# One-hot dispatch tables in paired 16-bit columns, and a semaphore for the first block's rows

## The reference, cut to what matters

```python
for j in range(C):                     # layer 0: two rounds
    gate = (xf @ router_W[j] + router_b[j]) / TEMP
    _, ids = jax.lax.top_k(gate + gate_bias[j], TOPK)          # TOPK = 2
    sel = (ids[:, :, None] == jnp.arange(E)[None, None, :]).any(axis=1)
    weights = softmax(where(sel, gate, -inf))
    ...                                # experts, weighted sum, shared experts, rms norm
# layer 1
gate_scores, expert_idx = jax.lax.top_k(tokens @ gate_w.T, 2)
out = sum over experts of c[:, e] * (gelu(tokens @ W1[e].T + B1[e]) @ W2[e].T + B2[e])
```

## Time and profile before

| | us |
|---|---|
| median of 3 runs | 1989.68 (1987.65 to 1990.22) |
| profiled execution, its own time | 1987.42 |
| its span | 1985.6 |
| TensorE busy (matmul) | 1745.8, 88% |
| VectorE busy | 1407.0, 71% |
| ScalarE busy | 1031.1, 52% |
| GpSimd busy | 828.3, 42% |
| mean granted clock of TensorE | 0.944 |

### The profile page before, as it was taken

How to read it: one execution, slowest core, us unless ns; L and a number is a source line. 1 busy time by engine, 2 the same in 40 slices (tenths; PEclk the granted TensorE clock), 3 DMA queues, 4 the chain that set the end, 5 groups by cost and what they waited for, 6 DMA issues and landing times. The chain is left out here.

```text
span 1985.6 us, 31822 instructions
## 1 busy us (share of the span) xinstructions
PE 1745.8 (88%) x11154; PEld 1543.6 (78%) x11154; DVE 1407.0 (71%) x2519; ACT 1031.1 (52%) x2084; POOL 828.3 (42%) x868
## 2 busy tenths in 40 slices
PE   5899999999999989999959899998389793999990
PEld 4788888888888878888848788887267682999990
DVE  4665465456434988777757987776799787788876
ACT  4344334334323434655555355554587462888882
POOL 2132232232222114777721257776231141888840
PEclk9999999999998999999979999999699885999995
DMA  4100000000012331666653236664700023788858
GB/s 159 64 1 11 11 5 5 11 11 0 11 57 93 110 114 55 211 191 197 196 175 124 76 112 192 194 185 152 250 33 1 1 75 122 232 276 274 268 176 264
DMA packets 147065, 233.01 MB, mean 117 GB/s; under 512 B 28162, under 2 KB 103172, under 8 KB 141956
## 3 DMA queue, kind: packets, MB, share of 16 engines
q1 hardware_dynamic: 123332, 167.04, 25.7%
q0 software_dynamic: 23616, 64.52, 10.9%
HBM read 175.65 MB, written 55.33 MB: 116 GB/s over the span
## 5 line engine op out<-in xcount | busy, mean ns | idle before, releaser
L183 POOL TENSOR_TENSOR spare_g<-neg_half 128x1 f32<-128x1 f32 x80 | 22.9, 287 | 577.6 <-ACT a_sg L553 141.3
L172 PE MATMUL bank<-gT_hi,w_hi 128*128 128x512 f32 x592 | 244.5, 413 | 0.0
L172 PE MATMUL bank<-gT_hi,w_lo 128*128 128x512 f32 x592 | 235.9, 398 | 0.0
L172 PE MATMUL bank<-gT_lo,w_hi 128*128 128x512 f32 x592 | 234.9, 397 | 0.0
L1817 POOL DMA_INDIRECT got<-b_rows,b_gather_i x168 | 170.7, 1016 | 65.8 <-issue 50.6
L1607 DVE TENSOR_TENSOR gT_lo<-bank,gT_hi 128x512 fp32r<-128x512 f32 x148 | 97.0, 690 | 132.7 <-ACT gT_hi L1430 102.4
L1460 ACT ACTIVATE m_hi<-gs 128x512 fp32r<-128x512 f32 x116 | 73.0, 633 | 124.1 <-DVE gs L1614 67.6
L172 PE MATMUL bank<-w_hi,m_hi 128*128 128x256 f32 x464 | 131.2, 283 | 5.2 <-DVE sent L1636 5.2
L172 PEld LDWEIGHTS bank<-gT_hi,w_lo 128*128 128x128 f32 x592 | 112.4, 190 | 27.2
L172 PE MATMUL bank<-w_lo,m_hi 128*128 128x256 f32 x464 | 131.0, 282 | 0.0
L172 PE MATMUL bank<-w_hi,m_lo 128*128 128x256 f32 x464 | 130.7, 282 | 0.0
(11 more groups left out here) (455 smaller groups left out, 5721.4 us busy)
## 6 DMA issues: line engine op xcount, KB each, us to landing
v_raw<-in_units SPq DMA_DIRECT2D x39, 1024.0 KB, 5.3
w_raw<-in_units SPq DMA_DIRECT2D x56, 256.0 KB, 4.0
shared<-in_units SPq DMA_DIRECT2D x40, 256.0 KB, 3.4
b_rows<-x SPq DMA_DIRECT2D x16, 512.0 KB, 3.1
got<-b_rows SPq DMA_DIRECT2D x16, 512.0 KB, 4.4
close_back<-b_kept SPq DMA_DIRECT2D x16, 512.0 KB, 6.2
d_back<-d_kept SPq DMA_DIRECT2D x16, 512.0 KB, 8.7
w_raw<-b_folded SPq DMA_DIRECT2D x26, 256.0 KB, 4.3
```

The lines of the kernel that those rows point to most:

```text
L172: ins = pe.matmul(out, a, b, start=first and n == 0, stop=last and n == of - 1)
L183: eng.tensor_tensor(b.spare_g[:, i:i + 1], b.neg_half[:, 0:1], b.neg_half[:, 0:1], ALU.mult)
```

## The change

Numbers and tables of the dispatch get a new layout and a new type. The 16 columns of a quarter are 8 runs of 2 (HOT_RUNS, HOT_RUN), and each table is laid out [partition, run, number, 2], so that the same number of two neighbouring columns lies side by side. The column numbers 0 to 127 and 0 to 83 are kept as bf16 and doubled (`iota_h`, `iotaq_h`), the turn numbers as bf16 (`turn_h`), and `in_h`, `at_h` are bf16. All three products of a quarter are made by VectorE: hot_at, hot_in, and the whole turn half of hot_id. GpSimd's hot is gone in layer 0, and so are ScalarE's single-column activations in layer 1. TensorE reads the tables with a step of two elements. Three conversions are added to `tables_vector`. In layer 1 the first two gathers, block 0's rows, signal `first_rows`, for which turn(0) waits.

```diff
-TURN_COLS = 8
+HOT_RUN, HOT_RUNS = 2, PICKS * N // P // 8
+def hot_numbers(table):
+    return table.unsqueeze(1).broadcast_to([P, HOT_RUNS, table.shape[1], HOT_RUN])
+def hot_cols(values, n):
+    return values.rearrange("p (a b) -> p a b", b=HOT_RUN).unsqueeze(2).broadcast_to([P, HOT_RUNS, n, HOT_RUN])
...
@@ b_tensor, inverse @@
-            ins = pe.matmul(B[6][:, 0:2 * NQB], b.hot_in[:, col, :], b.hot_id[:, col, :, :].rearrange("p a q -> p (a q)"), start=col == 0, stop=col == COLS // 4 - 1)
+            run, at = col // HOT_RUN, col % HOT_RUN
+            ins = pe.matmul(B[6][:, 0:2 * NQB], b.hot_in[:, run, :, at], b.hot_id[:, run, :, :, at].rearrange("p a q -> p (a q)"), start=col == 0, stop=col == COLS // 4 - 1)
...
@@ tables_vector @@
+    v.tensor_copy(b.iota_h, spread(b.disp[:, DISP["iota"]], HOT_RUN)).then_inc(link.sem, 1)
+    v.wait_ge(link.sem, link.next())
+    v.tensor_copy(b.iotaq_h, spread(b.disp[:, DISP["iotaq"]], HOT_RUN)).then_inc(link.sem, 1)
+    v.wait_ge(link.sem, link.next())
+    v.tensor_copy(b.turn_h, b.disp[:, DISP["turn"]]).then_inc(link.sem, 1)
+    v.wait_ge(link.sem, link.next())
...
@@ hot_vector @@
-    v.tensor_tensor(b.hot_at[:, :, :], mid(b.disp[:, DISP["iotaq"]][:, 0:NQB], COLS // 4), spread(b.at_f[:, cs], NQB), ALU.is_equal).then_inc(r.hot_at.sem, 1)
-    v.tensor_tensor(b.hot_in[:, :, :], mid(b.disp[:, DISP["iota"]], COLS // 4), spread(b.in_f[:, cs], P), ALU.is_equal).then_inc(r.hot_in.sem, 1)
+    v.tensor_tensor(b.hot_at, hot_numbers(b.iotaq_h[:, 0:NQB, :]), hot_cols(b.at_h[:, cs], NQB), ALU.is_equal).then_inc(r.hot_at.sem, 1)
+    v.tensor_tensor(b.hot_in, hot_numbers(b.iota_h), hot_cols(b.in_h[:, cs], P), ALU.is_equal).then_inc(r.hot_in.sem, 1)
+    v.wait_ge(r.hot_at.sem, r.hot_at.at(4 * rnd + j))
+    v.tensor_tensor(b.hot_id[:, :, 0], b.hot_at, hot_cols(b.turn_h[:, cs], NQB), ALU.mult).then_inc(r.hot_turn.sem, 1)
...
@@ b_gpsimd @@
-        g.tensor_tensor(b.hot_id[:, :, 0, :], b.hot_at[:, :, :], spread(b.disp[:, DISP["turn"]][:, cs], NQB), ALU.mult).then_inc(r.hot_turn.sem, 1)
-    for j in range(4):
-        hot(j)
...
@@ dispatch_vector: the same three operations, for all 16 columns of a quarter @@
-        v.tensor_tensor(b.hot_id[:, mine, 0, :], b.hot_at[:, mine, :], spread(table("turn")[:, mine], nq), ALU.mult).then_inc(r.hot_turn.sem, 1)
+        v.tensor_tensor(b.hot_id[:, runs, 0], b.hot_at[:, runs], hot_cols(b.turn_h[:, cs], nq), ALU.mult).then_inc(r.hot_turn.sem, 1)
...
@@ dispatch_scalar @@
-        for col in range(cs.start + TURN_COLS, cs.stop):
-            act.activation(b.hot_id[:, col, 0, :], b.hot_at[:, col, :], ACT.Copy, scale=float(col))
...
@@ d_gpsimd, gathers @@
-            g.indirect_dma_start(b.got[n % 6][:, c, :], None, rows, bass.IndirectOffsetOnAxis(b.gather_i[:, q:q + 1], 0)).then_inc(r.gathered[n % 6].sem, 16)
+            landed = r.first_rows if q < QBD else r.gathered[n % 6]
+            g.indirect_dma_start(b.got[n % 6][:, c, :], None, rows, bass.IndirectOffsetOnAxis(b.gather_i[:, q:q + 1], 0)).then_inc(landed.sem, 16)
...
@@ d_tensor, turn @@
-        pe.wait_ge(r.gathered[n % 6].sem, r.gathered[n % 6].at(n // 6, 16 * gathers_of(n)))
+        if k == 0:
+            pe.wait_ge(r.first_rows.sem, r.first_rows.at(0))
+        else:
+            pe.wait_ge(r.gathered[n % 6].sem, r.gathered[n % 6].at(n // 6, 16 * gathers_of(n)))
```

More of the change, by code:

```diff
@@ L1463, in hot_part @@
         act.wait_ge(r.hot_at.sem, r.hot_at.at(4 * rnd + j))
-        act.activation(b.hot_id[:, :, 1, :], b.hot_at[:, :, :], ACT.Copy, scale=b.disp[:, DISP["p1"]]).then_inc(r.hot_part.sem, 1)
+        act.activation(b.hot_id[:, :, 1], b.hot_at, ACT.Copy, scale=b.disp[:, DISP["p1"]]).then_inc(r.hot_part.sem, 1)
     for j, now, after, third in turn_steps(rnd):
@@ L1803, in b_gpsimd @@
 def b_gpsimd(g, b, s, r, dram, rnd):
-    def hot(j):
-        cs = slice(j * COLS // 4, (j + 1) * COLS // 4)
-        g.wait_ge(r.hot_at.sem, r.hot_at.at(4 * rnd + j))
-        g.tensor_tensor(b.hot_id[:, :, 0, :], b.hot_at[:, :, :], spread(b.disp[:, DISP["turn"]][:, cs], NQB), ALU.mult).then_inc(r.hot_turn.sem, 1)
     def gathers(k):
@@ L2460, in dispatch_tensor @@
         for col in range(j * COLS // 4, (j + 1) * COLS // 4):
-            ins = pe.matmul(b.bank[2][:, 0:2 * nq], b.hot_in[:, col, :], b.hot_id[:, col, :, :].rearrange("p a q -> p (a q)"), start=col == 0, stop=col == COLS - 1)
+            run, at = col // HOT_RUN, col % HOT_RUN
+            ins = pe.matmul(b.bank[2][:, 0:2 * nq], b.hot_in[:, run, :, at], b.hot_id[:, run, :, :, at].rearrange("p a q -> p (a q)"), start=col == 0, stop=col == COLS - 1)
     ins.then_inc(r.inverse.sem, 1)
@@ L2466, in dispatch_scalar @@
     for j in range(4):
-        cs = slice(j * COLS // 4, (j + 1) * COLS // 4)
+        runs = slice(j * HOT_RUNS, (j + 1) * HOT_RUNS)
         act.wait_ge(r.hot_at.sem, r.hot_at.at(j))
-        for col in range(cs.start + TURN_COLS, cs.stop):
-            act.activation(b.hot_id[:, col, 0, :], b.hot_at[:, col, :], ACT.Copy, scale=float(col))
-        act.activation(b.hot_id[:, cs, 1, :], b.hot_at[:, cs, :], ACT.Copy, scale=b.disp[:, DISP["p1"]]).then_inc(r.hot_part.sem, 1)
+        act.activation(b.hot_id[:, runs, 1], b.hot_at[:, runs], ACT.Copy, scale=b.disp[:, DISP["p1"]]).then_inc(r.hot_part.sem, 1)
 W1, W2 = KD * HID, KH * D
@@ L2820, in dispatch_buffers, with hot_buffers @@
             b.where = sb(scope, n + "where", [P, E, NT])
-            b.slot_f, b.in_f, b.at_f = (sb(scope, n + what, [P, COLS]) for what in ("slot_f", "in_f", "at_f"))
+            b.slot_f = sb(scope, n + "slot_f", [P, COLS])
+            b.in_h, b.at_h = (sb(scope, n + what, [P, COLS], BF16) for what in ("in_h", "at_h"))
             b.slot_i, b.in_i, b.at_i = (sb(scope, n + what, [P, COLS], I32) for what in ("slot_i", "in_i", "at_i"))
             b.found, b.source, b.padding = (sb(scope, n + what, [P, w]) for what, w in (("found", 2 * nq), ("source", nq), ("padding", nq)))
-        def hot_buffers(scope, name, nq, cols):
-            b.hot_in, b.hot_at = sb(scope, name + "_hot_in", [P, cols, P], BF16), sb(scope, name + "_hot_at", [P, cols, nq], BF16)
-            b.hot_id = sb(scope, name + "_hot_id", [P, cols, 2, nq], BF16)
+        def hot_buffers(scope, name, nq, runs):
+            b.hot_in, b.hot_at = sb(scope, name + "_hot_in", [P, runs, P, HOT_RUN], BF16), sb(scope, name + "_hot_at", [P, runs, nq, HOT_RUN], BF16)
+            b.hot_id = sb(scope, name + "_hot_id", [P, runs, 2, nq, HOT_RUN], BF16)
         with ExitStack() as sc:
@@ L2892, in program @@
             with ExitStack() as e:
-                hot_buffers(e, "d", NQD, COLS)
+                hot_buffers(e, "d", NQD, 4 * HOT_RUNS)
             with ExitStack() as e:
```

21 lines of the change are left out of this document (13 added, 8 removed).

## The result

The changed kernel takes **1976.13 us** (median of 4 runs, 1973.78 to 1978.16) against 1989.45 us of the kernel before in the same sessions (4 runs, 1987.65 to 1990.22). The ratio is 0.9936, with a 95% interval of 0.9924 to 0.9948. The forecast was 1976.0. The profiled execution took 1976.89 us with a span of 1975.0 us; that of before had 1985.6.

A forecast was written before the change was run, and what follows sets the result against it. Layer 0's expert rounds were taken as bound by TensorE, the last dispatch by VectorE's one-hot tables. 6.85 + 1.95 + 3.6 + 2.1 - 0.85 = 13.65 us off 1989.68 gave 1976.0 us, range 1971.0 to 1983.5.

The forecast's parts named there:

- VectorE's tables: One-hot tables: all-16-bit pairs run at half the slope; last dispatch quarters 2.58 us instead of 4.29, 6.85 us less in all.
- the part on the clock: Last dispatch: denser matmuls may bring the full clock, last 16 take 1.1 us less, later matmuls perhaps gain 1 to 2.
- Rounds 0 and 1: Layer 0, turn behind inverse(0): faster tables and product start it 3.6 us earlier in round 0, 2.1 in round 1.
- The new wait on the found copy: Round 1's turn: TensorE would wait 1.4 us for VectorE's copy of the found rows out of bank 6.
- The stalled join: Round 0: VectorE's 2.21 us for two joins included waiting for GpSimd's product; 0.92 us goes with it.
- Table copies: Three conversions in round 0's second step, ahead of the gT_lo that TensorE's gate matmul awaits: 0.85 us more.
- The upper end of 1.2 us: Table copies' cost in round 0 if the broadcast source runs at one element a cycle.
- First block's rows: Layer 1's experts: with turn(0) waiting only for the second gather, up(0) starts 1.95 us earlier, counted in full.
- everything up to the end hangs on the gathers: Last dispatch: the reason given for counting all 6.85 us of the tables as on the path.
- if a step between the rounds and the end does not hang on TensorE: Stated sign that the forecast is wrong, alongside a matmul column-time factor above 1.15 for the gap.
- Steps of two elements: TensorE's matmuls reading tables with a gap, rounds 0 and 1 and last dispatch: no cost; gap-paid rivals 0.06 and 0.05.
- k: Factor on TensorE's matmul column time from reading tables with a gap; taken as 1, with 2 as upper bound.

The follow-up runs named there:

- experiment 6: Changed kernel with runs of one column instead of two, so 16-bit operands without pairs: 1997.5 us, ratio 1.0042 to the kernel before.
- experiment 8: Changed kernel with the turn product of layer 0's rounds back on GpSimd, on 16-bit pairs: 1978.4 us, ratio 0.9944.
- experiment 9: Changed kernel with layer 0's turn product back on GpSimd (16-bit pairs) and VectorE's hot_in put ahead of hot_at: 1982.04 us, ratio 0.9963.
- Experiment 5: Changed kernel with the three table copies moved from the second step of round 0 to the fifth: 1973.82 us, ratio 0.9922.
- experiment 1: Changed kernel without the first rows' own semaphore, so turn(0) waits for all four gathers: 1975.0 us, ratio 0.9932.
- experiment 2: Changed kernel with gathers four groups ahead instead of six in layer 1's experts: 1971.44 us, ratio 0.9914.
- experiment 3: Changed kernel with gathers four groups ahead in layer 1's experts and without the first rows' own semaphore: 1975.9 us, ratio 0.9931.
- experiment 4: Kernel before the change with gathers four groups ahead instead of six in the last layer, nothing else: 1989.16 us, ratio 1.0001.
- experiment 7: Changed kernel with runs of four columns instead of two, so TensorE steps 8 bytes instead of 4: 1985.35 us, ratio 0.9976.
- experiment 11: Changed kernel run once more with nothing edited: 1973.14 us, ratio 0.992.

## Why the prediction was right, and where it was wrong

**VectorE's tables: right.** The three durations (0.85, 1.22, 0.80 forecast; 0.86, 1.22, 0.80 measured) and the cause (pairs, experiment 6) hold. The last dispatch gained the 6.85 us of the sum. In four of nine profiles with runs of two it gained another 1.0, because the last 16 matmuls ran at the full clock (1.29 us instead of 2.24), as the part on the clock allowed.

**Rounds 0 and 1: right, with the mechanism.** The turn came 3.71 and 2.14 us earlier for forecasts of 3.6 and 2.1. The new wait on the found copy was named beforehand, at 1.4 us in round 1 alone; it is 0.93 and 0.86. In round 0 TensorE's own chain did not end with the copy, as the step took it, because its clock no longer fell behind the shorter wait: 1.38 us for the 16 matmuls against 2.40.

**The stalled join: right.** Experiments 8 and 9 bring it back. The Trainium skill ("SBUF — State Buffer", section "SBUF: two separate sides") says that a VectorE operation with two SBUF inputs and a GpSimd operation that reads SBUF exclude each other for a whole instruction. The traces agree. The join's first part ended 0.55 us behind the product's end wherever the product ran, with 1.06 and 1.05 us of overlap (1.60 us long) and with 1.27 us (1.82 us long).

**Table copies: a mis-sized term.** The step read a wait of 0.85 us and booked 0.85 us. The wait came (0.77 us), and with it a granted clock of 0.83 instead of 1.00 from 680 to 690 us and 1.5 us more. Experiment 5 returned both. The upper end of 1.2 us was the wrong kind of bound: it varied the copies' durations, not what a wait does to TensorE.

**First block's rows: the step failed.** Up(0) did come 2 us earlier. The sentence that failed stands in the part on the tables, "everything up to the end hangs on the gathers", taken over for the first rows as if it held for every chain behind them. What was next late was not asked for GpSimd's queue, where 28 gathers precede the first scatter. It takes 1.95 us out of the sum. The prediction had named this as a sign of being wrong ("if a step between the rounds and the end does not hang on TensorE"), and it came, although the number was met. The trace of before had a sign of it, one wait of 0.9 us of `d_sent` on a scatter, which the prediction did not read. That the queue was the limit is shown by experiments 1 to 4.

**Steps of two elements: nearly right.** k is 1.05, so the 16 matmuls cost 0.05 us; eight quarters make at most 0.4 us where the sum had nothing. The argument "a pair still lies within 4 bytes" fits this and experiment 7, which shows how close the edge was.

**Why the sum still met the median.** The edited stretches make +2.3 - 3.7 - 2.1 - 6.85 + 0.2, -10.2 us. Two more things come from the other profiles. From round 1's turn to the transposes of `mod` that begin layer 1 the nine profiles with runs of two take 270.3 to 270.8 us, the two with the old tables 271.3 and 271.4: some 0.8 us gained beside the later quarters, which the prediction had at nothing. And the last dispatch is 1.0 us shorter in four of the nine. That makes about 11.4 us, against 13.3 us between the medians here and 15.5 in the session of experiment 11, whose intervals reach from 10.3 to 15.1 us and from 13.1 to 18.5. I had 1.95 too much for the first rows and 1.5 too little for the copies, so the edited stretches gave 3.5 us less than the 13.65 of the sum. The median met the forecast through gains that the sum did not have and through the scatter of the medians, which is luck. Whether 2 us more come from a place that I haven't found stays open.

**The 2.9 us between the rounds and the last dispatch:** scatter for the most part. From the first transposes of `m_hn` to the count matmuls on `d_picked`, where no kernel differs, eleven profiles of kernels made from the changed one gave 230.1 to 233.5 us, 231.2 in the first; the two of kernels made from the one before gave 233.2 both. That leaves scatter as the likely cause, with only two profiles on the side of before. The first stretch, up to the cast of `ones_r`, scatters in the same way: 671.8 to 674.6 us in the thirteen profiles, 671.81 and 674.05 in the two with the old tables. And the stretch from the count matmuls to round 0's first `hot_at` takes 12.0 to 12.1 us instead of 11.3 in experiments 2, 6, 7 and 11, with a granted clock of 0.86 in it instead of 1.00, though no edit touches it.

## What to carry to other kernels

A transfer or a first block that comes earlier is worth nothing until each queue that it feeds has been followed to its next wait. Here two chains ended within half a microsecond of each other, and two edits that each measured about 0 alone gave 2.2 us together. A wait of TensorE of under a microsecond isn't priced by its length; look at the granted clock behind it. Nor does every wait lower it: behind the 1.41 us before round 0's inverse the granted clock stayed at 1.00. And when VectorE reads one value per column, adjacent pairs in all operands halve the table's time, as long as TensorE then steps over no more than 4 bytes.
